# Patch convolution front of a vision tower: one source array in four transfers, weights centred in five pieces, and a new order of GpSimd's sums

## The reference, cut to what matters

```python
# token stage; x is (64, 3, 84, 84); C = 256, patches 14x14, windows of 3x3 patches, 4 windows per image
pe   = conv(x, conv_w, stride=(14, 14))            # 588 inputs -> 256 channels per patch
red  = mean of pe over the 9 patches of a window
win  = the 9 patches of each window
q    = LN(red) @ la_wq ;  k, v = split(LN(win) @ la_wkv)
local_out = red + softmax(q.k) v @ la_proj_w + la_proj_b
cls, patches = global attention of a class token over the 4 windows, and local_out @ mod_w + mod_b
h = concat(patches, cls)                            # (64, 5, 256)
h = h + two_delta_attention_layers(layernorm(h))    # 2 layers with feed-forward parts
h = h + fp4_feed_forward(layernorm(h))              # weights and inputs rounded in blocks of 16 (FP4)
```

## Time and profile before

| | us |
|---|---|
| median of 3 runs | 342.16 (340.58 to 342.92) |
| the profiled execution | 342.89 |
| its span, first to last instruction | 341.1 |
| DMA wait at the head of the chain that ended last | 9.19 |
| busy: PE / DVE / ACT / POOL | 288.6 / 208.4 / 98.9 / 36.7 |
| PE's mean granted clock, share of full speed | 0.93 |

### The profile page before, as it was taken

How to read it: one execution, slowest core, us unless ns; L and a number is a source line. 1 busy time by engine, 2 the same in 40 slices (tenths; PEclk the granted TensorE clock), 3 DMA queues, 4 the chain that set the end, 5 groups by cost and what they waited for, 6 DMA issues and landing times.

```text
span 341.1 us, 9674 instructions
## 1 busy us (share of the span) xinstructions
PE 288.6 (85%) x4388; PEld 216.2 (63%) x4388; DVE 208.4 (61%) x404; ACT 98.9 (29%) x200; POOL 36.7 (11%) x32
## 2 busy tenths in 40 slices
PE   0799999994999999757899998945889998698875
PEld 0466677683898976546876765725877775465452
DVE  3127879979777149555553488563562263599891
ACT  1023211320000147850232424881114232303210
POOL 0673100269100012000000000000000000000000
PEclk9999999999799999967978999996795999599997
DMA  8999990000000000000002106000000000000001
GB/s 180 262 239 322 281 393 4 2 0 0 0 2 0 3 1 2 0 4 2 0 4 69 58 0 262 2 0 4 2 2 5 0 0 0 0 3 0 0 0 38
DMA packets 2666, 18.29 MB, mean 54 GB/s; under 512 B 457, under 2 KB 777, under 8 KB 1873
## 3 DMA queue, kind: packets, MB, share of 16 engines
q1 hardware_dynamic: 2641, 17.93, 17.5%
HBM read 17.60 MB, written 0.33 MB: 53 GB/s over the span
## 4 chain that ended last, share of the span: by engine, by line
PE 69%; DVE 20%; ACT 4%; issue 3%; DMA 3%; SPq 0%; DVEq 0%; ACTq 0%
PE ps L1121 12%; PE ps L1412 11%; PE ps L1275 6%; PE ps L1165 4%; PE ps L1488 3%; PE ps L1618 3%; PE ps L1497 3%; DMA big<-in_patches 3%; PE ps L1179 2%; PE ps L1584 2%; PE ps L1111 2%; PE ps L1507 2%; PE ps L1537 2%; DVE big L997 2%; DVE wt L994 1%
## 5 line engine op out<-in xcount | busy, mean ns | idle before, releaser
L1121 PE MATMUL ps<-big,cwb 120*128 120x384 f32 x120 | 42.3, 505 | 10.6 <-DMA big<-in_patches 10.6
L1121 PEld LDWEIGHTS ps<-big,cwb 120*128 120x128 f32 x120 | 23.3, 197 | 25.2 <-issue 12.1
L1488 PE MATMUL ps<-wt,big 32*32 32x32 f32 x1280 | 17.2, 212 | 10.1 <-DVE wt L972 7.5
L1412 PE MATMUL ps<-xT,wl 128*128 128x320 f32 x88 | 24.3, 432 | 0.0
L280 POOL TENSOR_TENSOR xs<-xs,big 120x640 f32<-120x640 f32 x14 | 23.2, 1659 | 4.1 <-DMA big<-in_patches 3.0
L1275 PE MATMUL ps<-cst,ones 128*128 128x320 f32 x70 | 23.3, 475 | 0.0
L1488 PEld LDWEIGHTS ps<-wt,big 32*32 32x32 f32 x1280 | 15.2, 124 | 12.3 <-DVE wt L972 8.3
L1412 PEld LDWEIGHTS ps<-xT,wl 128*128 128x128 f32 x88 | 16.7, 190 | 7.0
L994 DVE COPY_PREDICATED wt<-cst,ps 128x320 f32<-128x320 int32 x16 | 8.1, 503 | 20.5 <-PE ps L1497 20.5
L336 ACT COPY pecT<-ps 128x384 f32<-128x384 f32 x12 | 5.7, 478 | 46.5 <-PE ps L1121 46.5
L1497 PE MATMUL ps<-wt,big 32*32 32x32 f32 x1280 | 15.5, 210 | 4.1 <-issue 4.1
(11 more groups left out here) (265 smaller groups left out, 522.3 us busy)
## 6 DMA issues: line engine op xcount, KB each, us to landing
big<-in_patches SPq DMA_DIRECT2D x6, 900.0 KB, 20.1
wl<-in_layers SPq DMA_DIRECT2D x2, 2176.0 KB, 25.3
wf<-in_ffn SPq DMA_DIRECT2D x1, 2112.0 KB, 26.8
wl<-in_layers SPq DMA_DIRECT2D x2, 1040.0 KB, 22.0
wt<-in_tok SPq DMA_DIRECT2D x1, 1536.0 KB, 39.1
wt<-in_tok SPq DMA_DIRECT2D x1, 768.0 KB, 14.1
cwb<-in_conv SPq DMA_DIRECT2D x1, 600.0 KB, 5.1
cst<-in_constants SPq DMA_DIRECT2D x1, 320.0 KB, 38.3
```

Of the source, the lines that this page charges most:

```text
L1121: last = mm(ps[:, i % 4, 0:GRP], cwc[:, k, c * P:(c + 1) * P], xg[:, g, k, :], start=(k == 0), stop=(k == KC - 1))
L1412: last = mm(ps[:, bank, 0:NT], w(c, j), x[:, c, :], start=(c == 0), stop=(c == CH - 1))
L1488: last = mm(ps[r, 4 + b, 32 * k:32 * k + 32], apm[r, NB * b + k, own], tc_[r, NB * b + k, :], start=True, stop=True)
```

## The change

The weights of the convolution and all patches are one source array, 120 rows of 51,200 bytes, and the two targets are one tensor `front` (the centred weights first, then the weights, then the groups). `LOADS` cuts the groups into four transfers: weights and group 0 (120 rows of 12,800 bytes), groups 1 and 2 (15,360), groups 3 and 4 (15,360), group 5 (7,680). Groups 1 and 2 now stand ahead of `vec` and `wt`; groups 3, 4 and 5 stand ahead of `wf`. The centring runs chunk by chunk and PE waits for each chunk within `conv(0, 0)`. POOL's order becomes `patch_sum` 0, 1, 2, then `square_sum(0)`, `patch_sum(3)`, `square_sum(1)`, `patch_sum(4)`, `square_sum(2)`, `patch_sum(5)`, then `square_sum` 3, 4, 5. DVE's order behind the centring is as before.

```diff
+LOADS = ((0, 1), (1, 3), (3, 5), (5, 6))
...
-        cwb = sb("cwb", [P, 2 * KC * C])
+        front = sb("front", [P, 2 * KC * C + 6 * KC * GRP])
+        cwb, big = front[:, 0:2 * KC * C], front[:, 2 * KC * C:]
...
-        cw = cwb[0:KP, 0:KC * C].rearrange("p (k n) -> p k n", k=KC)
-        cwc = cwb[0:KP, KC * C:].rearrange("p (k n) -> p k n", k=KC)
+        cwc = cwb[0:KP, 0:KC * C].rearrange("p (k n) -> p k n", k=KC)
+        cw = cwb[0:KP, KC * C:].rearrange("p (k n) -> p k n", k=KC)
...
-        s_x = [ctx.enter_context(nc.semaphore(f"s_patches{g}")) for g in range(6)]
+        s_load = [ctx.enter_context(nc.semaphore(f"s_patches{i}")) for i in range(len(LOADS))]
+        s_x = [s_load[i] for i, (first, end) in enumerate(LOADS) for g in range(first, end)]
...
-            sp.dma_start(cw[:, :, :], cw_d).then_inc(S["cw"], 16)
-            sp.dma_start(xg[:, 0], xp[0]).then_inc(s_x[0], 16)
-            sp.dma_start(xg[:, 1], xp[1]).then_inc(s_x[1], 16)
+            def patches(i):
+
+                at, end = (KC * (C + g * GRP) for g in LOADS[i])
+                if i == 0:
+                    at = 0
+                sp.dma_start(front[0:KP, KC * C + at:KC * C + end], xp[:, at:end]).then_inc(s_load[i], 16)
+
+            patches(0)
+            patches(1)
             sp.dma_start(vec[:, :], vec_d).then_inc(S["vecs"], 16)
             sp.dma_start(wt[:, 0:T_PR], wt_d[:, 0:T_PR]).then_inc(S["tokw"], 16)
-            sp.dma_start(xg[:, 2], xp[2]).then_inc(s_x[2], 16)
-            sp.dma_start(xg[:, 3], xp[3]).then_inc(s_x[3], 16)
+            patches(2)
+            patches(3)
             sp.dma_start(wf[:, :], wf_d).then_inc(S["ffnw"], 16)
-            sp.dma_start(xg[:, 4], xp[4]).then_inc(s_x[4], 16)
-            sp.dma_start(xg[:, 5], xp[5]).then_inc(s_x[5], 16)
...
             for g in range(3):
                 patch_sum(g)
-            for g in range(6):
+            for g in range(3):
                 square_sum(g)
+                patch_sum(3 + g)
             for g in range(3, 6):
-                patch_sum(g)
+                square_sum(g)
...
-            dve.wait_ge(S["cw"], 16)
-            v.tensor_reduce(cmean[:, :], cw[:, :, :], AX.X, ALU.add).then_inc(S["cwc"], 1)
-            dve.wait_ge(S["cwc"], 1)
-            v.tensor_scalar(cmean[:, :], cmean[:, :], 1.0 / C, None, ALU.mult).then_inc(S["cwc"], 1)
-            dve.wait_ge(S["cwc"], 2)
-            v.tensor_tensor(cwc[:, :, :], cw[:, :, :], cmean[:, :].unsqueeze(2).broadcast_to([KP, KC, C]),
-                            ALU.subtract).then_inc(S["cwc"], 1)
+            dve.wait_ge(s_x[0], 16)
+            for k in range(KC):
+                v.tensor_reduce(cmean[:, k:k + 1], cw[:, k, :], AX.X, ALU.add).then_inc(S["cwc"], 1)
+                dve.wait_ge(S["cwc"], 3 * k + 1)
+                v.tensor_scalar(cmean[:, k:k + 1], cmean[:, k:k + 1], 1.0 / C, None, ALU.mult).then_inc(S["cwc"], 1)
+                dve.wait_ge(S["cwc"], 3 * k + 2)
+                v.tensor_scalar(cwc[:, k, :], cw[:, k, :], cmean[:, k:k + 1], None, ALU.subtract).then_inc(S["cwc"], 1)
...
                 for k in range(KC):
+                    if i == 0:
+                        pe.wait_ge(S["cwc"], 3 * k + 3)
                     last = mm(ps[:, i % 4, 0:GRP], cwc[:, k, c * P:(c + 1) * P], xg[:, g, k, :],
                               start=(k == 0), stop=(k == KC - 1))
...
-            pe.wait_ge(S["cwc"], 3)
             conv(0, 0)
             conv(0, 1)
```

More of the change, by code:

```diff
@@ L56, with build @@
 TIE_DOWN = 1.0 - 2.0 ** -22
-def build(nc, xp, cw_d, vec_d, wt_d, wl_d, wf_d, cst_d, out):
+def build(nc, xp, vec_d, wt_d, wl_d, wf_d, cst_d, out):
     ctx = ExitStack()
@@ L79, in build @@
         ones = sb("ones", [P, P])
-        big = sb("big", [P, 6 * KC * GRP])
         pecT = sb("pecT", [P, CH, 18 * P])
@@ L202, in build @@
         wd = lw(L_D, C, FC)
-        once = """sqsum cw vecs consts tokw tokw2 ffnw cwc cmean9 ones conv copied squared xsum part redc redq var_mm rsr
+        once = """sqsum vecs consts tokw tokw2 ffnw cwc cmean9 ones conv copied squared xsum part redc redq var_mm rsr
             vec_mm vmean cls_v cls_mm cls_n kqb_mm kqb vb_mm vbias wkvg wqg q_mm q k_mm1 k_free stat_mm rk softmax score
@@ L1680 @@
     xp[:588] = x
-    xp = xp.reshape(KC, KP, 6, GRP).transpose(2, 1, 0, 3)
+    xp = xp.reshape(KC, KP, 6, GRP).transpose(1, 2, 0, 3)
     cw = np.zeros((KC * KP, C), np.float32)
@@ L1684 @@
     cw = cw.reshape(KC, KP, C).transpose(1, 0, 2)
+    xp = np.concatenate([cw.reshape(KP, -1), xp.reshape(KP, -1)], 1)
     def vector(w):
@@ L1710 @@
     wf = np.concatenate([rows(np.concatenate([a(f + "w_gate"), a(f + "w_up")], 0), 11), rows(a(f + "w_down"), CH)], 1)
-    arrays = {"in_patches": xp, "in_conv": cw, "in_vectors": vec, "in_tok": wt, "in_layers": wl, "in_ffn": wf,
+    arrays = {"in_patches": xp, "in_vectors": vec, "in_tok": wt, "in_layers": wl, "in_ffn": wf,
               "in_constants": constants()}
```

## The result

| | before | after |
|---|---|---|
| median of the runs, us | 342.5 (4 runs) | 350.12 (4 runs, 348.74 to 350.62) |
| ratio, with its 95% interval | | 1.0199 (1.015 to 1.0249) |
| span of the profiled execution, us | 341.1 | 348.1 |

The forecast was 347.3, slower. The direction came out, and so did the chain behind `wf`; one step in front of it did not. The size was 5.1 us in the forecast and 7.6 as measured.

A forecast was written before the change was run, and what follows sets the result against it. PE was taken as the bound from 10.59 to 73.58 us, DVE from 74.6 to 85.4. Terms: +7.6 (`wf`) +2.5 (POOL) −1.1 (slack) +1.7 (clock) −5.6 (patch sums) = +5.1, from 342.2 to 347.3 us; range 337.5 to 351.

The forecast's parts named there:

- Transfers: Loading: 120-row shape, not row length, limits the rate; merged transfers stay at 225 GB/s (bounds 222 and 400).
- rival 1: Loading: longer rows raise the rate to 400 GB/s, PE never waits at `red_var(0)`, 336 us; chance 0.19.
- The landing of `wf`: Loading: groups 4 and 5 ahead of it add 8.2 us, so it lands at 39.1 instead of 30.9.
- Front: Kernel start: centring after group 0 lands, beside POOL, delays PE by 2.0 us; covered later, so not in the sum.
- What waits behind `wf`: DVE to `red_var(0)`: `redc` 7.6 us late from `wf`, 2.5 more from POOL, less 1.1 slack: PE 9.0 late.
- DVE idles some 6 us: Sign (b): before line 588's first instruction DVE idles this long, released by the DMA of `wf` at about 39.
- (e): Sign after the patch sums move: lines 608, 609, 615 at 0.9 us each, PE's wait before line 1192 under 1 us.
- POOL's interference: DVE's lines 588 to 602 beside `patch_sum(5)`: 2.5 us later, between nothing and 4.6.
- the three lines that were named: DVE's lines 599, 601 and 602, each to sit out some 0.8 to 1.2 us of POOL's sums.
- Clock: PE behind its pause before `red_var(0)`: lowered clock costs 1.7 us, between 0 and 1.8.
- Given back: At 74 to 86 us: moved patch sums no longer hold DVE, returning 5.6 us, between 4.2 and 6.0.
- The sum: Whole kernel: all terms together make it 5.1 us slower, 347.3 us against the median 342.2.

The follow-up runs named there:

- e1: The changed kernel with `wf` sent ahead of the last transfer (group 5): 349.36 us, 1.0222 times the kernel before.
- e2: The changed kernel with POOL's order of before (square sums 0 to 5, then patch sums 3 to 5): 353.39 us, 1.0316 times before.
- e5: The changed kernel with the patch array padded from 120 to 128 rows of the same length: 345.18 us, 1.0056 times before.
- e4: The kernel before with POOL's patch sums 3 to 5 moved behind square sum 2: 336.69 us, 0.983 times before.
- e3: The changed kernel with POOL's order of before and `wf` ahead of groups 3 to 5: 345.71 us, 1.0107 times before.
- e6: The kernel before with weights and patches padded to 128 rows: 340.66 us, 0.9917 times before.
- e8: e3 with the convolution's weights again their own transfer ahead of group 0, still centred in pieces: 344.31 us, 1.0029 times before.
- e9: The changed kernel with 11 unread matrix products on PE in front of `red_var(0)`: 346.49 us, 1.0126 times before.

## Why the prediction was right, and where it was off

- **Transfers.** Right: row length changed nothing, the rate stayed at 219 to 237 GB/s, and rival 1 fell. The landing of `wf` was mis-sized: 42.15 us against 39.1. The term took 225 GB/s from windows. From landing to landing, groups 3 and 4 took from 22.1 (`wt`, issued at 2.09, 20.0 us to landing) to 31.3 (POOL's start), 1.84 MB in 9.2 us, 200 GB/s. The trace of before had shown it: its groups 2 and 3 landed 4.6 and 4.3 us behind the transfer ahead of them, 8.9 us where the term has 8.2. In all `wf` came 11.2 us later. Of these 9.4 are the two more groups, 1.1 is `wf` itself (6.3 us behind group 5's landing at 35.8, against 5.2 behind group 3's at 25.7 before), and 0.6 lies ahead of them, in groups 1 and 2, `vec` and the first part of `wt`. Why `wf` itself took longer is open.
- **Front.** Taken as 2.0, between 0.9 and 3.1. PE started 1.9 us late. Chunks one and two were held by POOL's two sums, the third was not:

```profile
11.07 0.15 DVE L655 TENSOR_SCALAR cmean<-cmean 120x1 f32<-120x1 f32 x1
11.26 1.10 DVE L657 TENSOR_SCALAR front<-front,cmean 120x256 f32<-120x256 f32 x1
...
14.53 0.35 DVE L657 TENSOR_SCALAR front<-front,cmean 120x256 f32<-120x256 f32 x1
```

- **What waits behind `wf`.** The chain was right link by link (DVE's joins, ACT's square, `red_var(0)`), but the step "DVE idles some 6 us" failed. It laid POOL's sums only beside lines 588 to 602, behind the wait, and took the time in front as empty, although its own timetable had POOL busy from 29.8 to 38.8 us. POOL was busy there beside DVE's key weights, and DVE, 8.1 us slower through them, used the pause up: 0.68 us of waiting. Had one cover been gone, the other would have cost nearly the same (e1, e2); the closing sentence, that every term but (e) hangs on when `wf` lands, was wrong. Behind the wait POOL's interference was 2.2 us of the predicted 2.5, but on lines 597 and 599 (before: 590 and 592), not on the three lines that were named: the size was luck. `red_var(0)` was late by 11.8 us instead of 9.0. The later `wf` explains that difference, but it wasn't needed for most of it: with `wf` at 36.8, ahead of the forecast's 39.1, `red_var(0)` still started at 49.6 (e1), 11.1 us late.
- **Clock.** Taken as 1.7 from the pause of 4.81 us. The pause was 9.67 us and the clock stayed low until 57 us: 3.5 us on lines 1141, 1152 and 1130 (1.01 + 1.92 + 5.11 against 0.34 + 0.97 + 3.23). This and `wf` are the two mis-sized terms. The longer pause isn't the whole reason: in e5 one of 5.66 us cost 3.3 us (last section). The price was read from a single case and carried over.
- **Given back.** Predicted 5.6. PE's lateness fell from 15.3 us (58.44 against 43.17 at the keys) to 9.4 at `project(0)`: 5.9. e4 shows the same gain by itself, 5.7.
- **The sum.** 11.8 + 3.5 − 5.9 = 9.4 at `project(0)`. The span grew by 7.0: the profile of before spent 2.4 us more behind that point. The largest part, 1.6 us, is the last twelve matrix products, with the granted clock at 0.82 and 0.77 in 333 to 336 and 336 to 341 us of before, and at 1.00 and 0.89 in 341 to 344 and 344 to 348 us of the change:

```profile
333.78 4.52 PE L1639 MATMUL ps<-wdT,big 128*64 128x256 f32 x12 [0.67 <-ACT big L559]
342.35 2.95 PE L1647 MATMUL ps<-wdT,front 128*64 128x256 f32 x12 [0.67 <-ACT front L566]
```

  Five of the twelve profiles show the long form of it (4.4 to 4.5 us), with no order by what was edited, and behind `project(0)` they take between 244.6 and 248.9 us. So the sum up to that mark was short by 4.3 us (5.1 against 9.4). That the profiled span grew by only 1.9 us more than forecast is in part such chance.

## What to carry to other kernels

A wait can have two covers. Before a cause is called the cause, ask what the waiting engine would do if the wait were gone, in front of it as well as behind; here taking either away left the time where it was or made it longer. A helper engine's work that holds up a busy one belongs where nobody waits for that one: the same sums cost 5.7 us at 74 us against their place at 39 us, and delayed the window means by 9.8 us at 31 us. And before transfers are merged for longer rows, compare the rate of other shapes in the same trace.

## What the runs showed of the hardware

- Which DVE instructions a POOL sum holds (lines as in the change): an addition with two inputs from SBUF even of one column (line 786, 128x1: 1.39 us in the change, 0.16 before), a scaling of 44 columns (line 597, 1.43 against 0.19), but not a scaling of a single column (line 655, 0.15 in the middle of POOL's first sum), a reduction (0.59 throughout), or an instruction with an input from PSUM and one from SBUF (0.69 throughout).
- After a pause of 4.8 us or more PE's instructions ran at half the clock (granted 0.50) for some microseconds, and the length of the pause alone doesn't set the price. From `red_var(0)` to the keys before took 4.5 us with no pause in front; behind pauses of 5.66 (e5), 6.23 (e2), 7.93 (e1) and 9.67 us (the change) it took 3.3, 2.1, 3.0 and 3.3 us more. Behind the pause of 4.8 us at `gathered`, the way to `project(0)` took 1.2 to 2.5 us more than the 6.9 of the kernels without it (e2, e3, before, e6, e8). Products that nobody reads, put into the longest pause, held the granted clock at 1.00.
- PE's first twenty convolution instructions took 8.4 us in some kernels and 9.6 in others with the same code and no wait between them (e4 and e6 had 9.64). The change's 8.6 became 9.5 in e1 and e2 and 10.0 in e9, with the same front. A single profile's front can't be trusted to better than 1.2 us.
